# A three-block kernel: q interleaved by pairs of chunks, v loaded as 48 rows with its two parts side by side

## The reference

```python
x = x + 0.5 * ffn(layernorm(x), ffn_weight, ffn_bias)
x = x + attn(layernorm(x), qkv_w, qkv_b, rpb, proj_w, proj_b)
x = x + 0.5 * ffn(layernorm(x), ffn_weight, ffn_bias)
```

```python
qkv = (x @ qkv_w.T + qkv_b)...           # q, k, v; q is scaled
kg, vg = k[:, :, nbr, :], v[:, :, nbr, :] # 13 neighbours of each token
attn = softmax(einsum('bhld,bhlkd->bhlk', q, kg) + rpb[:, bidx])
out = einsum('bhlk,bhlkd->bhld', attn, vg) @ proj_w.T + proj_b
```

## Time and profile before

| | |
|---|---|
| median of 3 runs | 3381.41 us |
| profiled execution: own time | 3373.88 us |
| profiled execution: span | 3372.0 us |
| PE busy | 3001.5 us, 89% |
| DVE / ACT / POOL busy | 68% / 56% / 57% |
| mean granted clock | 0.962 of full speed |
| DMA, 16 engines | 43.4% of their span, 449.44 MB |

### The profile page before, as it was taken

The page is one execution under the profiler, slowest core; times in us unless marked ns, Lnnn a source line. Parts: engine busy times, 40 slices in busy tenths (PEclk is TensorE's granted clock), DMA queues, the critical chain, the costliest instruction groups (busy, mean ns, idle before and its releaser), DMA issues. The chain is left out here.

```text
span 3372.0 us, 68516 instructions
## 1 busy us (share of the span) xinstructions
PE 3001.5 (89%) x24864; PEld 1829.5 (54%) x24864; DVE 2306.3 (68%) x3170; ACT 1888.3 (56%) x2323; POOL 1911.1 (57%) x1497
## 2 busy tenths in 40 slices
PE   0399999999999999999978999999999999499999
PEld 0244444444444444444447877777777776244444
DVE  7467666666666766666556666666666665799995
ACT  2355555555555555556545666665666666566662
POOL 3354554554455455445326666666666665788883
PEclk9699999999999999999978999999999999699999
DMA  2123233323323323332247767677767674344442
GB/s 76 63 88 113 88 113 113 107 93 115 119 92 113 113 94 106 113 113 95 93 127 187 191 189 191 189 185 194 188 181 194 187 192 117 115 151 149 149 148 86
DMA packets 339610, 449.44 MB, mean 133 GB/s; under 512 B 23048, under 2 KB 254496, under 8 KB 331168
## 3 DMA queue, kind: packets, MB, share of 16 engines
q1 hardware_dynamic: 339360, 445.57, 43.4%
HBM read 243.85 MB, written 201.38 MB: 132 GB/s over the span
## 5 line engine op out<-in xcount | busy, mean ns | idle before, releaser
L761 DVE TENSOR_TENSOR fq_out_lo<-fq_val,fq_out_hi 128x512 f16<-128x512 f32 x384 | 460.7, 1237 | 289.8 <-ACT fq_out_hi L829 289.8
L946 PE MATMUL fq_acc<-fq_y_hi_t,w_qkv 128*128 128x512 f16 x2048 | 614.6, 379 | 1.6 <-ACT fq_y_hi_t L842 1.6
L1186 ACT ACTIVATE att_ctx<-att_o_ps 32x512 f32<-32x512 f32 x512 | 300.9, 588 | 365.0 <-PE att_o_ps L1295 358.7
L829 ACT CAST fq_out_hi<-fq_val 128x512 f16<-128x512 f32 x384 | 237.3, 618 | 319.1 <-DVE fq_val L758 311.0
L1270 PE MATMUL att_s_ps<-att_k,att_q_bd 128*128 128x44 f16 x6144 | 388.4, 217 | 26.2 <-DMA att_q_bd<-q_parts 16.9
L1270 PEld LDWEIGHTS att_s_ps<-att_k,att_q_bd 128*128 128x128 f16 x6144 | 382.1, 170 | 27.0 <-issue 26.0
L946 PE MATMUL fq_acc<-fq_y_lo_t,w_qkv 128*128 128x512 f16 x1024 | 388.5, 379 | 0.0
L946 PEld LDWEIGHTS fq_acc<-fq_y_hi_t,w_qkv 128*128 128x128 f16 x2048 | 200.1, 98 | 243.6 <-ACT fq_y_hi_t L842 1.8
L946 PE MATMUL fq_acc<-w_qkv,fq_y_hi_t 128*128 128x512 f16 x1024 | 304.9, 380 | 16.7 <-ACT fq_val L824 16.7
L966 PE MATMUL fq_acc<-w_ffn,fq_f_hi_t 128*128 128x512 f16 x1024 | 310.7, 386 | 1.4 <-DVE fq_f_lo_t L806 1.4
L632 PE MATMUL ffn_acc<-w_ffn,ffn_hi_t 128*128 128x512 f16 x1024 | 306.8, 381 | 4.5 <-DVE ffn_x_ring L518 4.4
(11 more groups left out here) (188 smaller groups left out, 6510.2 us busy)
## 6 DMA issues: line engine op xcount, KB each, us to landing
att_v<-v_parts SPq DMA_DIRECT2D x96, 704.0 KB
att_k<-k_parts SPq DMA_DIRECT2D x64, 524.0 KB, 7.1
fq_x<-in_L_attn_x SPq DMA_DIRECT2D x32, 1024.0 KB, 6.8
x_after_ffn<-fq_x SPq DMA_DIRECT2D x32, 1024.0 KB, 4.3
att_q_bd<-q_parts SPq DMA_DIRECT2D x512, 64.0 KB, 3.8
att_x<-x_after_ffn SPq DMA_DIRECT2D x32, 1024.0 KB, 5.9
x_after_attention<-att_x SPq DMA_DIRECT2D x32, 1024.0 KB, 9.2
ffn_x_ring<-x_after_attention SPq DMA_DIRECT2D x32, 1024.0 KB, 6.3
```

The lines of the kernel that those rows point to most:

```text
L761: dve.tensor_tensor(out=out[1][:, b], in0=val[:, b % RING], in1=out[0][:, b], op=ALU.subtract).then_inc(s["out_lo"], 1)
L829: act.copy(out[0][:, b], val[:, b % RING]).then_inc(s["out_hi"], 1)
L946: op = pe.matmul(acc[:, b % RING], w, m, start=(kc == 0 and (a, c) == (0, 0)), stop=(kc == KC - 1 and (a, c) == PARTS[-1]))
L1186: return act.activation(ctx_f[rows, u.u % 2].rearrange("p g (c q) -> p g c q", q=CHUNK), o_ps[rows, :, :, h, :], ACT.Copy, scale=1.0 / P_UP)
```

## The change

Two layouts are changed, and the code that writes and reads them.

Queries: in `q_bd` the chunks of half a group are no longer interleaved by eight but by two, the two chunks of a pair. A column of a chunk's weights stands every 2 elements (4 bytes) instead of every 8 (16 bytes). A half of a group is loaded with 16 DMAs (four heads by four pairs, both parts in one) instead of 8 (four heads by two parts). A contiguous run of the copy is 64 elements, 128 bytes, instead of 256 elements, 512 bytes; each DMA moves 256 such runs, 32 KB. The DRAM tensor of q is laid out as [128, 32 groups, 2 parts, 4*512], and the eviction on ACT (L824) reorders by 8 pairs instead of by 2 halves: the same number of elements in a pattern of 2 by 32 by 8 instead of 8 by 32 by 2, innermost first.

Values: the two parts of a row stand side by side in DRAM, so that one run is 2048 bytes for both, and 48 rows are loaded for a chunk instead of 44 (the four rows behind the window meet probabilities that are zero). One DMA of 48x16 runs of 2048 bytes brings both parts, one of 48x16 runs of 1024 bytes brings the high part again into partitions 48 to 95; before, three DMAs of 44x16 runs of 1024 bytes. The low part of the probabilities is written at column 48 instead of 44.

The matmuls are the same in number, order and shape. The diff (a line number of a step in the changed kernel is two to five higher than before):

```diff
@@ -48,6 +48,8 @@
 PAIRS = P // PAIR
 UNITS = TOKENS // P
 PCOLS = KC * 2 * WIN
+VROWS = 48
+VTAIL = VROWS - CHUNK - NS
 MASKED = -1e30
 LN_STEPS = 8
 LN_UP = 2.0 ** 11
@@ -205,7 +207,8 @@
                         for at in (0, NS + TOKENS):
                             sp.dma_start(scratch["k"][part, :, :, at:at + NS].rearrange("g p c -> p g c"),
                                          zeros[:, 0:KC * NS].rearrange("p (g c) -> p g c", g=KC)).then_inc(padded, 16)
-                            sp.dma_start(scratch["v"][part, at:at + NS, :], zeros[0:NS, :]).then_inc(padded, 16)
+                        for at, rows in ((0, NS), (NS + TOKENS, VTAIL)):
+                            sp.dma_start(scratch["v"][at:at + rows, part, :], zeros[0:rows, :]).then_inc(padded, 16)
 
                     sp.wait_ge(wb_masked, 1)
                     for h in range(HG):
@@ -717,7 +720,7 @@
 
                         need(sp, s["out_lo"], NB * u.n + KC)
                         for part in range(2):
-                            place = scratch["q"][part, :, bass.ds(u.n * KC * GROUP, KC * GROUP)]
+                            place = scratch["q"][:, bass.ds(u.n, 1), part, :].rearrange("p t n -> p (t n)")
                             sp.dma_start(place, out[part][:, 0:KC, :].rearrange("p g c -> p (g c)")).then_inc(
                                 out_stored[0], 16)
                         need(sp, s["out_lo"], NB * u.n + 2 * KC)
@@ -727,7 +730,7 @@
                                 out_stored[1], 16)
                         need(sp, s["out_lo"], NB * (u.n + 1))
                         for part in range(2):
-                            place = scratch["v"][part, bass.ds(u.n * GROUP + NS, GROUP), :]
+                            place = scratch["v"][bass.ds(u.n * GROUP + NS, GROUP), part, :]
                             sp.dma_start(place.rearrange("(s p) c -> p s c", p=P), out[part][:, 2 * KC:NB, :]).then_inc(
                                 out_stored[2], 16)
 
@@ -819,8 +822,8 @@
                         need(act, s["out_lo"], u.n * NB + b - RING + 1)
                         value, total = val[:, b % RING], acc[:, b % RING]
                         if b < KC:
-                            value = value.rearrange("p (a q c) -> p a q c", a=2, q=CHUNK)
-                            total = total.rearrange("p (a c q) -> p a q c", a=2, q=CHUNK)
+                            value = value.rearrange("p (a q c) -> p a q c", a=GROUP // PAIR, q=CHUNK)
+                            total = total.rearrange("p (a c q) -> p a q c", a=GROUP // PAIR, q=CHUNK)
                         act.activation(value, total, ACT.Identity, bias=k.qk_bias[:, b:b + 1],
                                        scale=(k.S_Q if b < KC else k.S_KV)).then_inc(s["qk_val"], 1)
                         need(act, s["qk_val"], u.n * ACT_BLOCKS + b + 1)
@@ -1001,8 +1004,7 @@
     CHUNKS = P // CHUNK
     ROWS = PAIRS * KC * 2
     QUNITS = UG // 2
-    QCHUNKS = QUNITS * CHUNKS
-    QCOLS = QUNITS * P
+    QPAIRS = QUNITS * PAIRS
     HALF = ROWS // PAIRS
     with ExitStack() as ctx:
         def sb(name, shape, dt):
@@ -1014,7 +1016,7 @@
         def sem(name):
             return ctx.enter_context(nc.semaphore("att_" + name))
 
-        q_bd = sb("q_bd", [P, 2, 2, KC, P, QCHUNKS], F16)
+        q_bd = sb("q_bd", [P, 2, QPAIRS, 2, KC, P, 2], F16)
         keys = sb("k", [P, 2, 2, KC, GROUP + 2 * NS], F16)
         vals = sb("v", [P, 2, GROUP // CHUNK, 2, C], F16)
         x = sb("x", [P, 2, UG, C], F32)
@@ -1059,11 +1061,12 @@
                         sp.wait_ge(s["q_zero"], half + 1)
                     for h in range(HG):
                         rows = slice(h * HEAD_DIM, (h + 1) * HEAD_DIM)
-                        columns = scratch["q"][:, rows, bass.ds(g.n * KC * GROUP, KC * GROUP)].rearrange(
-                            "a p (g n) -> p a g n", g=KC)[:, :, :, half * QCOLS:(half + 1) * QCOLS]
-                        for part in range(2):
-                            sp.dma_start(q_bd[rows, half, part, :, rows, :].rearrange("p g m c -> p g (m c)"),
-                                         columns[:, part]).then_inc(q_loaded[half], 16)
+                        columns = scratch["q"][rows, bass.ds(g.n, 1), :, :].rearrange(
+                            "p t a (g v n) -> v p (t a g) n", g=KC, n=PAIR)
+                        for pair in range(QPAIRS):
+                            sp.dma_start(
+                                q_bd[rows, half, pair, :, :, rows, :].rearrange("p a g m c -> p (a g) (m c)"),
+                                columns[half * QPAIRS + pair]).then_inc(q_loaded[half], 16)
 
                 def keys_in(g):
                     if not g.within(GROUPS):
@@ -1079,10 +1082,12 @@
                         return
                     need(sp, s["weighted"], (g.n - 1) * UG)
                     sp.wait_ge(s["v_zero"], 2)
-                    for part, at in ((0, 0), (0, WIN), (1, 0)):
-                        rows = scratch["v"][part, bass.ds(g.n * GROUP, GROUP + 2 * NS), :]
-                        windows = bass.AP(rows.tensor, rows.offset, [[C, WIN], [CHUNK * C, GROUP // CHUNK], [1, C]])
-                        sp.dma_start(vals[at:at + WIN, g.u, :, part, :], windows).then_inc(v_loaded[g.u], 16)
+                    rows = scratch["v"][bass.ds(g.n * GROUP, GROUP - CHUNK + VROWS), :, :]
+                    for at, parts in ((0, 2), (VROWS, 1)):
+                        windows = bass.AP(rows.tensor, rows.offset,
+                                          [[2 * C, VROWS], [CHUNK * 2 * C, GROUP // CHUNK], [1, parts * C]])
+                        sp.dma_start(vals[at:at + VROWS, g.u, :, 0:parts, :].rearrange("p w a c -> p w (a c)"),
+                                     windows).then_inc(v_loaded[g.u], 16)
 
                 def residual_out(g):
                     if not g.within(GROUPS):
@@ -1225,7 +1230,7 @@
                     u = t.back(LAG_P)
                     if u.within(UNITS):
                         need(pool, s["p_hi"], u.n + 1)
-                        pool.tensor_tensor(out=prob[:, u.u % 2, :, WIN:2 * WIN], in0=score[:, u.u % 4],
+                        pool.tensor_tensor(out=prob[:, u.u % 2, :, VROWS:VROWS + WIN], in0=score[:, u.u % 4],
                                            in1=prob[:, u.u % 2, :, 0:WIN], op=ALU.subtract).then_inc(s["p_lo"], 1)
                     u = t.back(LAG_S)
                     if u.within(UNITS):
@@ -1257,7 +1262,7 @@
                         pe.wait_ge(k_loaded[g.u], 16 * 2 * (g.h + 1))
                     half = place // QUNITS
                     if place % QUNITS == 0:
-                        pe.wait_ge(q_loaded[half], 16 * HG * 2 * (g.n + 1))
+                        pe.wait_ge(q_loaded[half], 16 * HG * QPAIRS * (g.n + 1))
                     for pair in range(PAIRS):
                         need(pe, s["biased"], (u.n - 1) * PAIRS + pair + 1)
                         for kc in range(KC):
@@ -1266,7 +1271,7 @@
                                 col = (kc * 2 + j) * WIN
                                 at = place * P + c * CHUNK
                                 for a, b in PARTS:
-                                    q = q_bd[:, half, a, kc, :, place % QUNITS * CHUNKS + c]
+                                    q = q_bd[:, half, place % QUNITS * PAIRS + pair, a, kc, :, j]
                                     op = pe.matmul(s_ps[:, pair, col:col + WIN], q, keys[:, g.u, b, kc, at:at + WIN],
                                                    start=(a, b) == (0, 0), stop=(a, b) == PARTS[-1])
                         op.then_inc(s["scored"], 1)
@@ -1284,7 +1289,7 @@
                 def weigh(u):
                     g, place = group(u)
                     if place == 0:
-                        pe.wait_ge(v_loaded[g.u], 16 * 3 * (g.h + 1))
+                        pe.wait_ge(v_loaded[g.u], 16 * 2 * (g.h + 1))
                     need(pe, s["out_first"], u.n + 1)
                     need(pe, s["out_second"], u.n + 1)
                     need(pe, s["context"], u.n)
@@ -1329,9 +1334,9 @@
     x1 = nc.dram_tensor("x_after_ffn", [TOKENS, C], F32).ap()
     x2 = nc.dram_tensor("x_after_attention", [TOKENS, C], F32).ap()
     scratch = {
-        "q": nc.dram_tensor("q_parts", [2, P, KC * TOKENS], F16).ap(),
+        "q": nc.dram_tensor("q_parts", [P, GROUPS, 2, KC * GROUP], F16).ap(),
         "k": nc.dram_tensor("k_parts", [2, KC, P, TOKENS + 2 * NS], F16).ap(),
-        "v": nc.dram_tensor("v_parts", [2, TOKENS + 2 * NS, C], F16).ap(),
+        "v": nc.dram_tensor("v_parts", [NS + TOKENS + VTAIL, 2, C], F16).ap(),
     }
     ins = dict(qkv_w=qkv_w, qkv_b=qkv_b, rpb=rpb, proj_w=proj_w, proj_b=proj_b, ffn_w=ffn_w, ffn_b=ffn_b)
     k = Consts()
```

## The result

| | before | after |
|---|---|---|
| median (lowest to highest), us | 3378.57 (3373.41 to 3384.6) | 3620.78 (3619.17 to 3624.67) |
| ratio, 95% interval | | 1.0718 (1.0696 to 1.0740) |
| span of the profiled execution, us | 3372.0 | 3622.7 |

The median of before is of four runs, the three behind the 3381.41 above and one more. The forecast was 3292, in a range of 3255 to 3400. The time is 242 us above before, on the other side.

What follows compares the result with a forecast made beforehand. PE was taken to bound attention, its score matmuls held by strided weight loads. Dense weights -113, start of attention +8 and DMA load +16 made -89 us: 3285 from the profiled 3373.9, 3292 as median, range 3255 to 3400.

Steps and rivals of the forecast that it cites:

- What bounds the kernel: Attention: PE sets the pace; its score matmuls, 60.2 ns apart, are bound by weight loads reading columns 16 bytes apart.
- Cases 2 and 5: Score matmuls: dense weights bring only 55.8 ns, 3363, chance 0.13; weight read isn't behind the 60.2 ns, 3389, chance 0.07.
- Step 1: Score matmuls in attention: weights read at a step of 4 bytes save 0.91 us a unit, 113 us in all.
- cap of 7.25 us a unit: Attention unit: the chain through ACT and POOL keeps it from going under 7.25 us, from 8.16.
- The ring: ACT and POOL with PE: from a unit's transposes to POOL's low part, 7.21 us, which the next unit's transposes need.
- Step 2: Start of attention: more query DMAs on SP delay the first scores and next queries; +8 us, between 4 and 16.
- Step 3: DMA engines in steady attention: smaller query packets load them to 93%, values add nothing; +16 us, bounds 0 to 35.
- Case 3: DMA engines: 128-byte packets cost as much as 512-byte ones, 26.6 ns; 3395, or 3529 at 35 ns; chance 0.15.
- Step 4: SP's issuing in the attention loop: 32 query DMAs at 0.62 us make 29 us of a group's 30.4; fits, barely.
- case 4: SP: each query DMA is held as in the slower half, 1.0 us, 38 us a group; 3507; chance 0.08.
- The sum: Whole kernel: -113 + 8 + 16 = -89 us, which gives a median of 3292.
- No cost: Eviction L824, shifted column of L1228, wider rows of v and stores: the changed patterns cost nothing, bounds ±2 us.

Runs made afterwards that it cites:

- e10: The queries' change alone (values as before), with the query DMAs left out after the first group: 3206.34 us, 0.9485 of before.

## Why the prediction was wrong, by its steps

**What bounds the kernel** and the weight read as the cause of the 60.2 ns: right, shown by the steps of 16, 8 and 4 bytes. Cases 2 and 5 fall.

**Step 1: right in kind, too small.** The gain in the steady state was put at 113 us by a cap of 7.25 us a unit. The unit went to 6.48, under it, and e10 brought 173 us. The cap counted 7.21 us from a unit's transposes to the end of a low part of POOL, "which the next unit's transposes need". They don't. ACT and POOL make the two parts of unit t-3 in the body in which PE transposes unit t-4. The stretch begins with the transposes of one body and ends with a low part of the next body, whose unit PE transposes in the body after that: two units later, not one. The timeline of PE, ACT and POOL in the changed kernel agrees:

```profile
2345.15 0.61 PE L1286 MATMUL att_t_ps<-ident,att_prob 128*128 128x128 f16 x8
...
2349.90 0.76 ACT L1201 CAST att_prob<-att_score 128x704 f16<-128x704 f32 x1
2350.74 1.89 POOL L1233 TENSOR_TENSOR att_prob<-att_score,att_prob 128x704 f16<-128x704 f32 x1
2351.62 0.61 PE L1286 MATMUL att_t_ps<-ident,att_prob 128*128 128x128 f16 x8
```

The same stretch is 2350.74 + 1.89 - 2345.15 = 7.48 us here, no shorter than before, and the next transposes start at 2351.62 while that low part still runs. The ring goes round in two units, not in one, and was no cap. A chain read from a timeline is a bound only if its last link is what the first one waits for; the units that the semaphores count say which.

**Step 2: the mechanism right, the size not.** Predicted +8 us, 4 to 16; the first scores come 6.6 us later and the first 12 units take 19 us more. With the values as before the first 12 units take +14 and with 8 query DMAs -10, so most of it goes with the number of query DMAs: the second burst of 32 takes 32.0 us where 16 took 15.48.

**Step 3: queries right, values wrong.** The packets of 128 bytes were put at 64 engine-us more a group (118 - 54); the queries' change alone has 439 - 384 = 55. Case 3's mechanism falls with it, though a loss came. The values were costed at nothing, 143 against 141. These two are at different prices: 141 is 2112 packets at 66.9 ns, 143 is 2.36 MB at the mean rate; at the mean rate for both it is 143 against 131, +12, still far from what came. 48 rows cost 129 to 142 engine-us more than 44 in three pairs of kernels, and 95, 113 and 148 us of time. I had noted that 48 rows go to more engines than 44, and drew "more evenly" from it, which changed no term. The trace says otherwise: a share of 1.04 for 113 GB/s, where 0.574 had brought 618 packets of 1 KB in 4.5 us, 141 GB/s. The Trainium skill's rule (DMA: Bandwidth & Descriptors, Why a DMA increments its semaphore by 16) that a DMA of 48 rows is spread over 16 engines and one of 44 over 11 agrees with the shares, 1.04 here and 0.57 there. But it says nothing of a price, and spreading was the loss here. The term should have had the bound that I gave every unseen thing elsewhere; the packets of 2 KB on all engines were seen nowhere before.

**Step 4 failed, and it decides the sign.** "29 us of 30.4. It fits, barely" took 0.62 us for each of 32 query DMAs, the pace of the half that isn't held, and 3 us for holding. Measured: 0.88 us in the queries' change alone, 1.09 in the changed kernel, so that a group is 38.5 and 42 us. Against the prediction's 20 + 3 + 4 + 2 = 29 us, SP's round in the queries' change alone is 2 x 11.14 = 22.3 for the issues, 17.07 - 11.14 = 5.9 more in the half behind the values, 6.8 for the values and 3.8 for the rest: 38.8. In the changed kernel it is 21.9 + 13.1 + 2.6 + 3.8 = 41.4. All four terms were short in the first and three in the second, the holding-up most of all.

That is the mechanism of case 4, which had 0.08 of the chance. Its 38 us a group and 3507 meet the 38.5 and 3506 of the queries' change alone in part by luck: it had 32 + 4 + 2 where 28.2 + 6.8 + 3.8 were measured, and it was meant for the changed kernel, which took 3621. What I gave against it, that the holding is a wait paid once per half, took its size for fixed at 3 us; it was 5.9 and 13.1. It doesn't grow with the number of issues either: with 4 DMAs instead of 16 for the same packets it is 14.10 - 6.50 = 7.6. What fewer issues save is the rest, 2 x 6.50 = 13.0 us instead of 22.3, and it is enough: -209 us for the same packets. A sum that fits "barely" on the resource whose price is least known, two rows 0.62 and 1.0 apart in the same view, deserved more than 0.08, and the range should have held its 3507.

**The sum.** Measured against before: queries' part +130 (of this -173 for the dense weights where no query is late, so some +303 for late queries and all that follows), values' part +96, and 16 for having both. The stalls also cost clock: 0.82 granted in the pass, against 1.00.

**No cost** held for the eviction: 773 ns on average, 772 before.

**Also missed:** the "issue" stall at the head of a pass. It was 2.9 us on average and I let it be. It is up to 12.5 us in the changed kernel, 4.1 us on average (53.3/13) with fast units and no queries, and 4.2 to 5.6 in the kernels with 8 query DMAs and 44 rows. So a faster unit lengthens it. The 48 rows alone don't (37.9/13 = 2.9); they add stalls elsewhere in the pass. Every trace has a queue of instructions on the same DMA engines (the page of before):

```profile
q8 instruction: 223, 3.65, 0.5%
```

Its packets of 16 KB tell what PE stands for. From 1900 to 2750 us, all 12 of PE's "issue" stalls of over 1 us in the kernel before end 1.6 to 1.8 us after such a packet has landed. So do all 34 with the values' change alone (1.3 to 1.8) and all 39 with 8 query DMAs and 48 rows (1.4 to 2.3), where chance would put 15 to 17% of moments 1.0 to 2.3 us behind a landing. So PE waits for code that comes through the DMA engines, and in these two, with 48 rows, it does so about three times as often as before. In the changed kernel it is all 18 (1.3 to 2.4). That the code is late because it stands behind the data is argued only; no run changes its fetch alone.

**Open:** why 48 rows make the packets dear (the one other distance in DRAM changed nothing; splitting recovers part); and why query DMAs are held while the engines are 71 to 77% busy, even with no values on their queue. That SP sets the pace of the changed kernel is shown by its round and the 8 DMAs; what holds it is not.

## What to carry to other kernels

Count issues beside packets and bytes: where a queue's burst shows two paces, cost a change that multiplies its DMAs at the slower one, and lay out DRAM so that one DMA brings what several did; that turned 3.8% slower into 2.3% faster here. The number of rows of a DMA is a parameter with a price of its own: compare the engines' share with the GB/s before and after such a change, not bytes. Before a chain of engines is taken for a cap, check by the units that its semaphores count that its end is what its start waits for.

The version to use is that of the 8 query DMAs with 44 rows side by side, 3277 us, or the same with four chunks interleaved, 3272.
